# Index score groups in the opposite order, and pair weights in every second step

## The reference, cut to what matters

```
iq = (h @ idx_wq_w).reshape(b, s, 16, 128);  ik = h @ idx_wk_w;  iw = h @ idx_weights_w * 16**-0.5
idx_scores = einsum('bqn,bnqk->bqk', iw, relu(einsum('bqnd,bkd->bnqk', iq, ik))) * 128**-0.5
idx_scores = where(causal, idx_scores, -inf);   topk_idx = top_k(idx_scores, 128)
scores = (q_nope . k_nope + q_pe . k_pe) * 192**-0.5, masked by causal and topk;  out = softmax(scores) @ v @ o_w
```

## Time and profile before

| what | us |
|---|---|
| median of 3 runs | 1595.93 |
| profiled execution, own time | 1594.58 |
| profiled execution, span | 1592.8 |
| busy in the span: PE, DVE, ACT, POOL | 1388.6, 1212.9, 830.9, 584.6 |

### The profile page before, as it was taken

How to read it: one execution, slowest core, us unless ns; L and a number is a source line. 1 busy time by engine, 2 the same in 40 slices (tenths; PEclk the granted TensorE clock), 3 DMA queues, 4 the chain that set the end, 5 groups by cost and what they waited for, 6 DMA issues and landing times.

```text
span 1592.8 us, 21704 instructions
## 1 busy us (share of the span) xinstructions
PE 1388.6 (87%) x7310; PEld 1134.7 (71%) x7310; DVE 1212.9 (76%) x2379; ACT 830.9 (52%) x1774; POOL 584.6 (37%) x557
## 2 busy tenths in 40 slices
PE   2765999999979868988555999999999999999987
PEld 1644788788868857767333778888888888888865
DVE  6545655565447879989995898888888888888864
ACT  3675322232224546555332666676666666676641
POOL 3432000000013235334223555555555555656522
PEclk9976899999989989988666999999999999999998
DMA  6553000000022145544541000000000000000021
GB/s 219 172 159 93 0 1 1 0 1 1 1 81 67 52 118 176 159 133 125 169 149 61 13 1 26 26 26 26 26 26 26 26 26 25 26 25 8 9 73 53
DMA packets 83724, 95.61 MB, mean 60 GB/s; under 512 B 11680, under 2 KB 59296, under 8 KB 83104
## 3 DMA queue, kind: packets, MB, share of 16 engines
q1 hardware_dynamic: 83616, 94.24, 19.1%
HBM read 75.34 MB, written 18.87 MB: 59 GB/s over the span
## 4 chain that ended last, share of the span: by engine, by line
PE 60%; DVE 23%; issue 3%; DMA 1%; ACT 1%; SPq 1%; DVEq 1%; POOL 0%; ACTq 0%
PE ps L305 14%; PE ps L307 13%; PE ps L306 13%; PE ps L1468 8%; DVE top L1113 4%; DVE acc L1103 4%; DVE acc L1116 4%; PE ps L1488 3%; PE ps L1487 3%; PE ps L1282 2%; DVE rop L1177 1%; DVE xn_l L1163 1%; PE ps L1506 1%; PE ps L1505 1%; DVE rop L1176 1%
## 5 line engine op out<-in xcount | busy, mean ns | idle before, releaser
L571 POOL TENSOR_SCALAR pm<-pm,smx 128x128 f32<-128x128 f32 (+7 forms) x256 | 190.0, 750 | 214.3 <-DVE smx L1157 214.3
L803 ACT ACTIVATE pm<-pm,smx 128x128 f32<-128x128 f32 (+7 forms) x256 | 197.2, 773 | 36.5 <-DVE smx L1151 34.9
L1151 DVE CUSTOM_DVE_ANT_0 pm<-ps,mbias 128x128 f32<-128x128 f32 (+7 forms) x256 | 191.3, 752 | 29.3 <-PE ps L307 14.3
L1468 PE MATMUL ps<-ident,pm 128*128 128x128 f32 x1152 | 171.6, 276 | 7.8 <-DVE xn_l L1163 3.9
L809 ACT ACTIVATE xn_h<-ps 128x512 fp32r<-128x512 f32 (+3 forms) x256 | 127.6, 511 | 92.3 <-PE ps L1468 89.8
L1163 DVE TENSOR_TENSOR xn_l<-ps,xn_h 128x512 fp32r<-128x512 f32 (+3 forms) x256 | 144.6, 587 | 26.6 <-ACT xn_h L809 25.4
L1468 PEld LDWEIGHTS ps<-ident,pm 128*128 128x128 f32 x1152 | 133.0, 141 | 27.5 <-POOL pm L571 8.2
L305 PE MATMUL ps<-latT_l,qc_h 128*128 128x512 f32 (+3 forms) x384 | 142.5, 371 | 4.8 <-DVE rop L1177 3.6
L307 PE MATMUL ps<-latT_h,qc_h 128*128 128x512 f32 (+3 forms) x384 | 134.0, 349 | 0.0
L306 PE MATMUL ps<-latT_h,qc_l 128*128 128x512 f32 (+3 forms) x384 | 133.5, 348 | 0.0
L1103 DVE SCALAR_TENSOR_TENSOR acc<-relu,iw,acc 128x768 f32<-128x768 f32 (+4 forms) x105 | 109.9, 1089 | 16.2 <-ACT relu L734 16.2
(11 more groups left out here) (243 smaller groups left out, 3940.0 us busy)
## 6 DMA issues: line engine op xcount, KB each, us to landing
iwq_raw<-in_L_attn_idx_wq_w SPq DMA_DIRECT2D x48, 256.0 KB, 3.8
ow_raw<-in_L_attn_o_w SPq DMA_DIRECT2D x16, 512.0 KB, 3.7
wuvo<-pr_hl SPq DMA_DIRECT2D x16, 512.0 KB, 3.5
base<-in_L_ffn_mean_w SPq DMA_DIRECT2D x28, 256.0 KB, 2.8
wring<-in_L_ffn_w SPq DMA_DIRECT2D x24, 256.0 KB, 3.0
wq<-pr_hl SPq DMA_DIRECT2D x16, 256.0 KB, 2.2
wuvo_h<-wuvo SPq DMA_DIRECT2D x16, 256.0 KB, 2.6
wuvo_l<-wuvo SPq DMA_DIRECT2D x16, 256.0 KB, 2.9
```

The source lines that it names most:

```text
L571: pool.tensor_scalar(pm[:, i % 4, 0:w], pm[:, i % 4, 0:w], smx[:, 32 + i:33 + i], 0.0, ALU.mult, ALU.add).then_inc(hd_p, 1)
L803: act.activation(pm[:, i % 4, 0:w], pm[:, i % 4, 0:w], ACT.Exp, bias=smx[:, i:i + 1], scale=-1.0, accum_out=smx[:, 16 + i:17 + i]).then_in ...
L1151: dve.tensor_tensor_reduce(out=pm[:, i % 4, 0:w], in0=two_banks(2 * (i % 2), w), in1=mbias[:, TRI[t]:TRI[t + 1]], scale=1.0, scalar=3.0 * BIG,
L1468: done = pe.transpose(ps[:, 4 + i % 2, tile(k)], pm[:, tq % 4, tile(4 * c + k)], ident[:])
```

## The change

The groups run in the opposite order, (6, 7), (4, 5), (1, 2, 3). The groups with wide rows and two slots now come first, so n < 48 becomes n < 64 with the sides exchanged (`WIDE`). Fixed counts that hung on the order (48, 80, 112 and 45, 78, 110) are computed (`DONE`), and the wait of the first round for its tile's causal cut counts by the tile's place in the order (`PLACE`). `PAIR_AT` has 13 pairs instead of 11: from step 20 to 34 one in every second step, then steps 37, 39, 41, 43, 46. The list behind step 47 has three pairs instead of five, and SP's list there is adapted.

```
-INDEX_TILES = ((1, 2, 3), (4, 5), (6, 7))
-INDEX_COLS = ((P, 512), (512, 768), (768, 1024))
+INDEX_TILES = ((6, 7), (4, 5), (1, 2, 3))
+INDEX_COLS = ((768, 1024), (512, 768), (P, 512))
+PLACE = {t: k + 1 for k, t in enumerate(sum(INDEX_TILES, ()))}
+DONE = [IDXH * sum(map(len, INDEX_TILES[:k + 1])) for k in range(3)]
+WIDE = DONE[1]
-PAIR_AT = {20: 0, 23: 1, 26: 2, 29: 3, 32: 4, 34: 5, 37: 6, 39: 7, 42: 8, 44: 9, 47: 10}
+PAIR_AT = {20: 0, 22: 1, 24: 2, 26: 3, 28: 4, 30: 5, 32: 6, 34: 7, 37: 8, 39: 9, 41: 10, 43: 11, 46: 12}
+LATER = len(PAIR_AT)
...
-            return 2 + n % 4 if n < 48 else 2 + 2 * (n % 2)
+            return 2 + n % 4 if n >= WIDE else 2 + 2 * (n % 2)
...
-            return n - 3 if n < 48 else max(48, n - 1)
+            return max(WIDE, n - 3) if n >= WIDE else n - 1
...
-            store_pair(8)
-            load_pair(10)
-            store_pair(9)
-            for j in range(10, PAIRS):
+            store_pair(11)
+            load_pair(LATER)
+            store_pair(12)
+            for j in range(LATER, PAIRS):
...
-                pool.wait_ge(ix_acc, (48, 80, 112)[phase])
+                pool.wait_ge(ix_acc, DONE[phase])
...
-                        dve.wait_ge(ix_mask, t + 1)
+                        dve.wait_ge(ix_mask, PLACE[t] + 1)
...
-                    dve.wait_ge(tk_rep, (45, 78, 110)[phase] + k + 1)
+                    dve.wait_ge(tk_rep, DONE[phase] - len(INDEX_TILES[phase]) + k + 1)
```

More of the change, by code:

```diff
@@ L326, in score_bank @@
         def score_bank(n):
-            return 2 + n % 4 if n < 48 else 2 + 2 * (n % 2)
+            return 2 + n % 4 if n >= WIDE else 2 + 2 * (n % 2)
         def relu_slot(n, w):
-            return relu[:, n % 4 // 2, 512 * (n % 2):512 * (n % 2) + w] if n < 48 else relu[:, n % 2, 0:w]
+            return relu[:, n % 4 // 2, 512 * (n % 2):512 * (n % 2) + w] if n >= WIDE else relu[:, n % 2, 0:w]
         def slot_free(n):
-            return n - 3 if n < 48 else max(48, n - 1)
+            return max(WIDE, n - 3) if n >= WIDE else n - 1
         def acc_of(t):
@@ L558, in _ @@
                     split_pair(PAIR_AT[step])
-            for j in range(11, PAIRS):
+            for j in range(LATER, PAIRS):
                 split_pair(j)
```

## The result

The changed kernel takes 1616.74 us (median of four runs, 1609.54 to 1622.3) where the kernel before takes 1595.95 (four runs, 1595.08 to 1597.21). The ratio is 1.013, with an interval from 1.0092 to 1.0168: slower by 15 to 27 us. The forecast of 1607.5 had the sign and the wait that decides, and was 9 us short: the likeliest case, slower by 5 to 19 us, was missed by 2 us, and the time lies inside the whole range (1582 to 1626).

The account below looks back on a forecast made before the run. VectorE was taken to set the pace, TensorE close behind. +10.4 us until step 20, +25.1 until step 47 and -23.9 in the tail made +11.6; 1606.2, plus 1.35 for the median, gave 1607.5 us, range 1582 to 1626.

Parts of the forecast that it names:

- the likeliest case: Whole kernel slower by 5 to 19 us, own range 1601 to 1615 us; chance 0.50.
- The decisive step: Pairs two steps apart: ScalarE's split waits for the previous pair's store, queued behind a load; ten waits instead of two.
- rival B: Worse chain: intervals of 17.5 us in the second group, 16 in the third, first group +12; 1622 us, chance 0.20.
- Steps 20 to 47: Second and third group: +25.1 us, though VectorE's floors grow only from 148.7 to 157.7.
- P12: End of the products of pair 12, the last before the tail; put at 793.8.
- the floors: VectorE's undisturbed time a step: 6.43 us in the second group (5.02 before), 5.37 in the third (5.90 before).
- the worst case: Every split and both GpSimd index roundings hit a sum: 2.4 + 2 x 1.3 us an interval, kernel some 1616.
- The chain: From one pair's products through store wait, split, copy, rounding and scoring to the next products: 15.1 to 15.6 us, 16.0 taken.
- Rival A: VectorE's longer steps hide the waits for the store: -8.7 us, 1587 us; chance 0.22.
- Rival C: Gain and loss cancel: first group +5, intervals of 15 and 13.8 us; 1596 us, chance 0.08.
- The tail: Behind step 47's rounding VectorE sets the end: 59.7 us instead of 83.6, giving 23.9 us back.
- the second side: In the tail, pairs, final weights and their store: 51.7 us from the last in-loop pair, covered by VectorE by 8.5 us.

Follow-up runs that it names:

- e1: Changed kernel with SP's store of a pair issued ahead of the load in the same step: 1588.53 us.
- e6: Changed kernel with GpSimd's split of a pair cut from 1024 to 16 columns: 1610.21 us.
- e3: Kernel before (old order of groups) with the new table of 13 pairs: 1633.64 us.
- e7: e1 with the 14 loads of final weights issued one a step from step 21 on, not all in step 20: 1579.74 us.
- e2: Changed kernel (new order of groups) with the old table of 11 pairs and SP's old list behind the loop: 1620.39 us.
- e5: e2 with SP's store of a pair issued ahead of the load in the same step: 1611.29 us.
- e8: e4 with the 14 loads of final weights issued one a step from step 21 on, not all in step 20: 1576.3 us.
- e4: Kernel before with SP's store of a pair issued ahead of the load in the same step: 1587.14 us.

## Why the prediction was right, and where it was short

**The decisive step held.** Ten waits and some 60 us were forecast, 59.6 measured, at the place in SP's order that was named; e1 takes away what makes them and nothing else, and 28 us go. Without them the kernel is not slower but faster than before. So the sign of the change hangs on them. The size, +20.8 us, is not that of the forecast's own case (slower by 5 to 19) but lies where rival B was priced; that the time falls into the stated range owes something to its width.

**The terms, one by one.** Step 0 to 16: +10.2 (forecast +9). Steps 16 to 20: +1.7 (+1.4). Steps 20 to 47: +30.0 (+25.1). From there to the last mask: -22.0 (-23.9). The sum is +19.9 in the stage where I had +11.6. The forecast positions look better than that, P12 at 794.20 (793.8) and the end at 856.70 (854.0), but the stage began 5.6 us earlier in that execution, so this closeness is luck.

From step 20 the mis-sized terms are two intervals. In us, the ow_raw issues of the changed kernel against the forecast: pair 0 to 1, 18.3 (13.6); the next five, 77.0 (80), 15.4 each; pair 6 to 7, 13.8 (14.5); 7 to 8, 24.2 (19.6); 8 to 9, 12.2 (13); 9 to 11, 29.6 (29); 11 to 12, 19.9 (19.6). Both long ones are collisions, with a scoring or products at a lowered clock behind them. The first has stood above. The second holds three steps, whose roundings take 21.7 us, the floors (16.1) and 5.6 of collisions, half of these in its first step; the other 2.5 come on TensorE, where after a pause of 2.19 us the granted clock was 0.50 from 727 to 732.5, and scoring and products took 3.0 and 3.7 us (1.7 and 2.1 at full clock). Its last step, at 717.53, on VectorE and GpSimd:

```profile
716.02 2.37 POOL L548 TENSOR_TENSOR pr_hl<-pr_out,pr_hl 128x1024 fp32r<-128x1024 f32 x1 [8.11 <-ACT pr_hl L763]
717.53 4.41 DVE L1107 SCALAR_TENSOR_TENSOR acc<-relu,iw,acc 128x256 f32<-128x256 f32 x3
718.36 3.02 POOL L535 TENSOR_TENSOR iwq_l<-iwq_raw,iwq_h 128x512 fp32r<-128x512 f32 x2
```

Three sums took 4.41 us of 1.66. I had given the first interval 0.7 us for collisions, because it has no wait; that no wait stands there doesn't keep the split and an index rounding off the same sums. In e6 the two intervals are 16.3 and 21.2, shorter by 2.0 and 3.0; the index roundings remain there. The Trainium skill, page "SBUF — State Buffer", section "Who interferes with whom", gives the rule (the two engines shut each other out for the whole instruction), and here the trace agrees: 2.64 us lost by the sums while they lay beside GpSimd's work for 3.6 us (the index rounding, 1.26 us alone, took 1.88 there), 2.75 in 3.9. It is not the worst case that I had priced by it (5.0 us an interval): behind a split that had waited, the sums lost some 1.9 us in the second group and 2.9 in the third.

**The chain.** Its bare length is 16.8 us in e3, not 15.1 to 15.6. The terms that were too small are the scoring (4.0 us, taken as 3.1 to 3.6) and the products (2.9, taken as 2.1). In the changed kernel the five intervals came out at 15.4 in the mean, but they are two kinds: 16.9 and 16.7, which are the bare chain's, then 14.8, 13.5 and 15.0. The short ones belong to short pauses of TensorE. Behind 3.5 and 3.2 us of pause the scoring took 4.0 us, behind 2.6 us 3.6, and behind 1.4 us 2.1, all of it at full clock:

```profile
675.14 0.47 PE L309 MATMUL ps<-ikT_l,iqT_h 128*128 128x512 f32 x1
...
677.28 0.34 PE L1404 MATMUL ps<-kvbT,qbT 128*128 128x64 f32 x2
```

```profile
675.00:679.50 4.50, 4.47 (x26) 3.12 (x26) 4.47 (x3) 3.82 (x9) 4.50 (x3) 1.00 0.10 27
```

VectorE's rounding behind the wait idled for 2.6, 1.1, 0.5, 0 and 0 us in the five, so from the fourth on VectorE had no slack left. So 16.0 is near the mean of two cases and not the length of either.

**Rival A** (longer steps hide the waits) is wrong in result. e1 shows what would have been left had they been hidden: steps 20 to 47 in 174.7 us, where I had worked out 175.4 for it. In the second group A was nearly right, which I had not seen: the waits cost only 94.9 - 87.9 = 7.0 us there, of 30.5 us of waiting. In the third they cost 105.7 - 86.8 = 18.9, of which 15.0 are collisions that e7 shows to return in part without any wait. My split of the loss between the groups was wrong the other way round: I had charged the second group with the stalls (intervals of 16), but even without them its steps and collisions need 88 us.

**Rival B** priced 1622 through intervals of 17.5. The run is nearer to it (1616.74) than to the centre. Of its terms one was half seen: a pause that costs a full scoring at the low clock level stands in the first stalled intervals (16.9 and 16.7), but the mean is 15.4, and the first group's +10.2 is short of its 12. **Rival C** is out.

**The tail.** VectorE ends it, as forecast, and the second side lies some 10 us earlier. e2 and e5 show what keeps it there: with five pairs left for the tail instead of three, the second side ends 16.0 us behind the last mask. Their expectations had said so (76 us against 60). The tail itself is 61.5 us, 1.8 over its term, by one collision: a sum of step 47 lost 2.1 us to the split of pair 12. In e2, e5 and e6, without it, the tail is 59.4.

**Two expectations missed in size.** e1 came out 9 us better than forecast; the collisions that went with the waits, 15.1 us, had not been counted. e2 came out 14 us worse, all of it between step 20 and step 47: +24.7 us where I had put +6, which is less than the floors alone (+9.0), and the collisions grew from 15.8 to 24.7 us.

**Left open.** The last four additions of the first layer, which no kernel here touches, began between 437.73 and 443.81 in the profiled executions; I have no experiment on that. The kernels also spread differently from run to run: the changed one over 12.8 us and e3 over 14.3, with ten waits each, but e6, with ten waits too, over 7.0, e1 without one over 9.2, and e8 over 3.2. What sets this spread isn't shown.

## What to carry to other kernels

Where a queue issues in a fixed order and a single buffer is emptied through it, check each pair of "load that waits for compute" and "store that frees the buffer" whenever the spacing changes: put the store first. Work that is moved out of a tail is only won if the steps that take it in have slack, and both sides of the tail have to shrink together (here selections on VectorE, and pairs with their stores). Before pricing a rearrangement, look for the queue blocks that it works around: two edits of SP's order, with the old order of groups, gave -21 us, where the whole rearrangement gave +21.

## What the runs showed of the hardware

A TensorE that had paused for some microseconds mostly came back at a lower granted clock in these runs (behind a pause of 1.4 us it stayed at 1.00, in the rows of the chain above), and that is a cost beside the pause. The scoring of tiles 4 and 5 took 2.1 to 2.2 us at a granted clock of 1.00 and 4.0 at 0.50, the products of a pair 2.1 and 3.7. It isn't the waits for the store alone that make such pauses. The second group shows 0.86 in the changed kernel with five waits and 0.87 in e2 with none, where TensorE paused three times for 5.0 to 5.6 us until VectorE had rounded; e1 shows 0.90. With the old order, whose steps are shorter, it shows 0.97 before, 0.93 in e4 (no wait in either) and 0.81 in e3 (five waits). From step 16 to 20 it is 0.83 in the kernel before, whose TensorE pauses for 11.30 us there, and 1.00 in e8.

Where a VectorE sum and a GpSimd instruction overlapped, the one that had begun later took the loss. GpSimd's rounding of index weights and two sums (896 and 1024 columns) of the first group of the changed kernel, twice:

```profile
502.83 3.37 DVE L1107 SCALAR_TENSOR_TENSOR acc<-relu,iw,acc 128x896 f32<-128x896 f32 x2
506.45 2.33 DVE L1107 SCALAR_TENSOR_TENSOR acc<-relu,iw,acc 128x896 f32<-128x896 f32 x2
```

```profile
503.51 1.60 POOL L535 TENSOR_TENSOR iwq_l<-iwq_raw,iwq_h 128x512 fp32r<-128x512 f32 x1 [2.70 <-ACT iwq_h L731]
508.30 1.65 POOL L535 TENSOR_TENSOR iwq_l<-iwq_raw,iwq_h 128x512 fp32r<-128x512 f32 x1 [3.18 <-ACT iwq_h L731]
```

The second rounding began 0.78 us into the last sum: the sums took their undisturbed 2.33 us, and the rounding 1.65, which takes 1.26 alone. The first began 0.37 us before the last sum, and that sum took 1.0 us more. Over the whole stage of the changed kernel 42 sums lay beside a split or a rounding for more than 0.2 us, 56.0 us together, and lost 34.0. So a shift by a fraction of a microsecond in one engine's start decides which of the two pays, and a shift by 2 us can decide whether they meet at all.
